# Spikes of the first feed-forward layer: eight GpSimd comparisons or two ScalarE activations

## The chip, the cores and the metric

The kernel runs on one core of one Trainium2 chip. The time is that of the device for one execution, in microseconds, from the first to the last instruction and what lies around them; lower is better.

## The reference

The input x has 16 sequences of 512 steps with 256 features. The first block projects x with Wr, Wk and Wv and runs each result through leaky neurons over time:

```
v = v + (x_t - v) * 0.5
s = (v - 1.0 >= 0)
v = v * (1 - s)
```

With the spikes r, k, v of the three it computes h = 0.9 h + k v and y = r h, projects y with Wo, adds x and normalises (x1). The feed-forward layer takes h1 = x1 W1 + b1 (1024 columns), runs it through the same neurons to the spikes s1, takes h2 = s1 W2 + b2, runs the neurons again, adds x1 and normalises; then x is added once more and normalised (x3). The second block is a mixture of 8 experts of 256 by 256 of which each token takes the best two, weighted by a softmax, added to x3 and normalised.

## The kernel before

Time is cut into 32 chunks of 16 steps; a chunk has 16 x 16 = 256 columns (step, sequence). Features lie on the 128 partitions. The kernel is a pipeline written out by hand: beat k (from -2 to 38) works at each stage on a chunk that is some beats behind. Beats 7 to 32 have all stages and are called steady (`edge` is false). All engines have their own instruction stream, ordered by `beat`, and wait for one another by semaphores with counts that depend on k.

The neurons of all layers run together on VectorE: `U` (two slots, used in turn) holds for each of the 16 steps 256 columns: 6 x 16 for r, k, v, 8 x 16 for h1, 2 x 16 for h2. Each step is one `membrane` (L710, U = 0.5 V + U) and one `reset` (L717, V = U where U is under the threshold). Halving is left out of the sums, so that the threshold is 2.0. Between these 32 instructions the lists STEADY, FILL and DRAIN place everything else that VectorE does, by slot numbers from 0 to 31. In STEADY the five steps of y stand in slots 0 to 4 (L747, L751, L757, L762, L766, L768), the sum z (L734) in slot 5, x3_low (L823) in slot 30.

y goes to TensorE, which multiplies it with Wo (`attn`, L378). TensorE's order in a steady beat: expert 0, the first of three r/k/v projections, attn, the transpose of z, the two other projections, w2 (L397, the product of the spikes s1 with W2), the transpose of x1, experts 1 to 3, w1, expert 4, the transpose of x3 (read by ScalarE as x3_hi, L534, and by VectorE as x3_lo, L823), the transpose of the gates, experts 5 to 7. Products are made with weights and data split in a high and a low part.

ScalarE moves the products out of PSUM: `to_lif` (L534 and L546) writes them into the slot of U for the next beat, `read_expert` (L583) writes weighted expert outputs to `term`, `normalised` (L597) applies the last layer norm, and L681 issues the DMA of the result. The beat of ScalarE begins with `to_lif` of the three projections, which waits for y, since it overwrites what y reads.

GpSimd's queue in a steady beat: the spikes s1 of the chunk (`spikes_h1`, eight instructions L1084, one for each 128 of the 1024 columns, 256 wide, from a strided view of U), then the DMA that adds term 4 of the chunk before to `acc` (`add_even`, L1102), the DMA that adds term 5 to `odd_sum` (`add_odd`, L1113), the bias on xb (`add_bias`, two instructions L1120), and between further DMAs the reciprocal deviations (L1070, L1072), the low part of x1 (L1127, two) and, last, the low part of x (L1091).

In the edge beats the spikes are made by VectorE (L1012).

Of the kernel before, what the change touches and what calls it, by code (L numbers as in the profile page):

```python
# [26 lines left out]
ALU = mybir.AluOpType  # L27
ACT = mybir.ActivationFunctionType

P = 128  # L30
B, T, D, F, E = 16, 512, 256, 1024, 8
STEPS = 16
N = STEPS * B
CHUNKS = T // STEPS
TILES = N // P
DK = D // P
FK = F // P
RKV_TILES = 3 * DK
EPS = 1e-5
THRESHOLD = 2.0  # L40
DECAY = 0.9


COL_H1 = RKV_TILES * B
COL_H2 = COL_H1 + FK * B
# [6 lines left out]
LAG_S = 3  # L52
# [54 lines left out]
class Beat:  # L107
# [15 lines left out]
    @property  # L123
    def dve_spikes(self):

        return FK if self.edge else 0

    def value(self, per, lag, add=0):

# [29 lines left out]
def some(n):  # L159

    return n > 0


def build(nc, x_T, x_tok, w_rkv, w_o, w_1, w_2, w_e0, w_e, consts, out):
    with ExitStack() as ctx:
        def sb(name, shape, dt=F32):
            return ctx.enter_context(nc.sbuf_tensor(name, shape, dt))

        def sem(name):
            return ctx.enter_context(nc.semaphore(name))  # L170


        wrkv_raw = sb("wrkv_raw", [P, 3, DK * D])
        wrkv_hi, wrkv_lo = sb("wrkv_hi", [P, 3, DK * D], F32R), sb("wrkv_lo", [P, 3, DK * D], F32R)
        wo = sb("wo", [P, DK, D])
        w1_hi, w1_lo = sb("w1_hi", [P, DK * F], F32R), sb("w1_lo", [P, DK * F], F32R)
# [8 lines left out]
        bias_stack = sb("bias_stack", [STACK, D], F32R)  # L185
        decay = sb("decay", [P, DK * B, STEPS])
        neg_half = sb("neg_half", [P, TILES])

        U = sb("U", [P, 2, STEPS, COLS])
        V = sb("V", [P, COLS])  # L190
# [60 lines left out]
        y_steps, attn_done, ln1_steps = sem("y_steps"), sem("attn_done"), sem("ln1_steps")  # L251
        x1T_done, x1_ready = sem("x1T_done"), sem("x1_ready")
        x1_hi_ready, x1_lo_ready = sem("x1_hi_ready"), sem("x1_lo_ready")
        s1_ready = sem("s1_ready")
        z_ready, zT_done, xb_ready = sem("z_ready"), sem("zT_done"), sem("xb_ready")
        ln2_steps, ln3_steps = sem("ln2_steps"), sem("ln3_steps")
        x3T_done, x3_hi_ready, x3_lo_ready = sem("x3T_done"), sem("x3_hi_ready"), sem("x3_lo_ready")
# [274 lines left out]
        def _(act):  # L532
# [3 lines left out]
            def to_lif(b, fill, col, tiles, bias):  # L536
# [11 lines left out]
                                                ACT.Identity, bias=cst[:, bias + e:bias + e + 1])  # L548
                last.then_inc(proj_read, 1)

            def read_x1(b):

                slot = b.slot(LAG_Y, 4)
                act.wait_ge(x1T_done, b.value(1, LAG_Y, 1))

                if some(b.value(2, LAG_Y + 4, 2)):
                    act.wait_ge(z_ready, b.value(2, LAG_Y + 4, 2))
                if some(b.fills()):
                    act.wait_ge(proj_filled, b.fills())
                for k in range(DK):  # L560
                    if k == 1 and b.has(LAG_M):
                        read_expert(b, 1)
                    for dst, done in ((x1_hi[:], x1_hi_ready), (x1[:, slot], x1_ready)):
                        nc.scalar.activation(dst[:, k, :], ps_attn[:, k, :], ACT.Identity,  # L564
                                             bias=cst[:, C_BE1 + k:C_BE1 + k + 1],
                                             scale=cst[:, C_G1 + k:C_G1 + k + 1]).then_inc(done, 1)
# [43 lines left out]
            def beat(b):  # L610
                if b.k == LAG_M:
                    act.wait_ge(split_lo, PIECES)
                fill = 0
                if b.has(LAG_RKV):

                    if b.has(LAG_Y):
                        act.wait_ge(y_steps, b.value(Y_STEPS, LAG_Y, Y_STEPS))
                    for f in range(3):
                        to_lif(b, f, 2 * f * B, 2, None)
                    fill += 3  # L620
                if b.has(LAG_M):

                    act.wait_ge(gate_steps, b.value(GATE_STEPS, LAG_M, 7))
                    nc.scalar.activation(gexp[:], gdiff[:], ACT.Exp).then_inc(gexp_ready, 1)
                if b.has(LAG_S):

                    if b.has(LAG_Z):
                        act.wait_ge(z_ready, b.value(2, LAG_Z, 2))
                    to_lif(b, fill, COL_H2, 2, C_B2)
                    fill += 1  # L630
                if b.has(LAG_Y):
                    read_x1(b)
                elif b.has(LAG_M):
                    read_expert(b, 1)
                if b.has(LAG_M):
                    read_expert(b, 2)
                if b.has(LAG_Y):

                    if b.has(LAG_S):
                        act.wait_ge(s1_ready, b.value(FK, LAG_S, FK))  # L640
                    for f in (0, 1):
                        to_lif(b, fill + f, COL_H1 + 2 * f * B, 2, C_B1 + 2 * f)
                if b.has(LAG_M):
                    read_expert(b, 3)
                if b.has(LAG_Y):
                    to_lif(b, fill + 2, COL_H1 + 4 * B, 2, C_B1 + 4)
                if b.has(LAG_Z):
                    norm_x3(b)
                if b.has(LAG_Y):
                    to_lif(b, fill + 3, COL_H1 + 6 * B, 2, C_B1 + 6)  # L650
                if b.has(LAG_M):
                    read_expert(b, 4)
                if b.k == LAG_RKV:
                    act.wait_ge(consts_loaded, 16)
                    copy(bias_stack[:], bias_raw).then_inc(bias_hi_ready, 1)
                    act.wait_ge(vec_set, 5)
                if b.has(LAG_Z):
                    act.wait_ge(x3T_done, b.value(1, LAG_Z, 1))

                    if some(b.value(E - 1, LAG_Z + 2, E - 1)):  # L660
                        act.wait_ge(expert_done, b.value(E - 1, LAG_Z + 2, E - 1))
                    copy(x3_hi[:, b.slot(LAG_Z, 2)], ps_zx[:]).then_inc(x3_hi_ready, 1)
                if b.has(LAG_M):
                    act.wait_ge(gateT_done, b.value(1, LAG_M, 1))
                    if some(b.value(1, LAG_M)):
                        act.wait_ge(bias_done, b.value(1, LAG_M))
                    copy(gate_T[:], ps_attn[0:STACK, :, 0:P]).then_inc(gateT_ready, 1)
                if b.has(LAG_X):
                    split_x(b)
                if b.k == LAG_X:  # L670
                    for f in range(3):
                        act.wait_ge(wrkv_loaded[f], 16)
                        copy(wrkv_hi[:, f, :], wrkv_raw[:, f, :]).then_inc(wrkv_hi_ready, 1)
                if b.has(LAG_M):
                    for e in (5, 6, 7):
                        read_expert(b, e)
                if b.has(LAG_F):
                    act.wait_ge(fin_steps, b.value(FIN_STEPS, LAG_F, FIN_STEPS))
                    normalised(3, res, res).then_inc(res_ready, 1)
                    act.wait_ge(res_ready, b.value(1, LAG_F, 1))  # L680
                    act.dma_start(out[b.chunk(LAG_F)], res[:]).then_inc(out_stored, 16)  # L681
                for p in pieces_in(b.k):
                    _, hi, _, n = pieces_of(p)
                    act.wait_ge(raw_loaded[p % RAW_SLOTS], 16 * (p // RAW_SLOTS + 1))
                    copy(hi, term[:, p % RAW_SLOTS, 0:n]).then_inc(split_hi, 1)
# [6 lines left out]
        def _(dve):  # L692
# [312 lines left out]

            def spikes_h1(b):


                if some(b.w2_fills()):
                    dve.wait_ge(proj_filled, b.w2_fills())  # L1010
                for ft in range(FK - b.dve_spikes, FK):
                    v.tensor_scalar(s1[:, ft, :].rearrange("p (t b) -> p t b", b=B),  # L1012
                                    U[:, (b.k - 1) % 2, :, COL_H1 + ft * B:COL_H1 + (ft + 1) * B],
                                    THRESHOLD, None, ALU.is_ge).then_inc(s1_ready, 1)

# [48 lines left out]
        def _(pool):  # L1064
# [6 lines left out]
                pool.wait_ge(rstd_ready[ln], b.value(2, lag, 1))  # L1071
                g.tensor_tensor(rstd[ln][:], veps[ln][:], neg_half[:], ALU.pow).then_inc(rstd_ready[ln], 1)  # L1072

            def spikes_h1(b, part):

                if part == 0:

                    if some(b.value(2 * STEPS, 0)):
                        pool.wait_ge(lif, b.value(2 * STEPS, 0))
                    if some(b.w2_fills()):  # L1080
                        pool.wait_ge(proj_filled, b.w2_fills())
                for e in range(2):
                    ft = 2 * part + e
                    last = g.tensor_scalar(s1[:, ft, :].rearrange("p (t b) -> p t b", b=B),  # L1084
                                           U[:, (b.k - 1) % 2, :, COL_H1 + ft * B:COL_H1 + (ft + 1) * B],
                                           THRESHOLD, None, ALU.is_ge)
                last.then_inc(s1_ready, 2)

            def split_x(b):
                pool.wait_ge(x_hi_ready, b.value(1, LAG_X, 1))  # L1090
                g.tensor_tensor(x_lo[:], xt[:, b.slot(LAG_X, 2)], x_hi[:].bitcast(F32),  # L1091
# [38 lines left out]
            def beat(b):  # L1130


                has_y, has_z, has_m, has_f = (b.has(lag) for lag in (LAG_Y, LAG_Z, LAG_M, LAG_F))
                if b.has(LAG_S):
                    for part in range((FK - b.dve_spikes) // 2):
                        spikes_h1(b, part)
                if has_f:
                    add_even(b, LAG_F, 4)
                    add_odd(b, LAG_F, 5)
# [26 lines left out]
                                    ALU.subtract).then_inc(split_lo, 1)  # L1166

            g.memset(neg_half[:], -0.5).then_inc(pool_set, 1)
            pool.wait_ge(pool_set, 1)
            run_beats(beat)  # L1170


# [43 lines left out]
```

## Time and profile before

| | |
|---|---|
| median of 3 runs | 1124.46 us (1119.31 to 1125.79) |
| the profiled execution | 1122.8 us |
| its span | 1120.9 us |
| VectorE busy | 1024.0 us, 91% |
| TensorE busy | 958.6 us, 86% |
| GpSimd busy | 715.7 us, 64% |
| ScalarE busy | 545.4 us, 49% |
| the eight spikes a beat, L1084 | 223.2 us in 208 instructions |
| mean granted clock of TensorE | 0.946 of full |

In the profile PE is TensorE, PEld its weight loads, DVE VectorE, ACT ScalarE, POOL GpSimd and SP the engine that only issues DMAs; a q behind a name is the engine's queue. The busy time of a GpSimd or VectorE instruction includes time in which it stands still for the other. Arrows read from input to output, leftwards: `s<-U` writes s from U. A time in brackets is how long the engine had been idle, with what ended it.

### The profile page before, as it was taken

To read this page: it belongs to the slowest core of one execution; us is meant where nothing else is said; L and a number is where in the kernel's file an instruction comes from. 1 tells how busy PE (TensorE), PEld (TensorE's weight loads), DVE (VectorE), ACT (ScalarE), POOL (GpSimd) and SP (SyncE) were. 2 spreads that over 40 slices of the span, in tenths; PEclk is the share of its full clock that TensorE was granted. 3 is DMA by queue.
4 is the path that set the end of the run, shared out by engine and by line. 5 is a ranking of instruction groups with operands and counts; after the bars stand their busy time and mean duration, and the time that the engine had idled before them with its cause. 6 is when DMAs were issued, how large, how long until landed. Compare 5 with 4: busy or idle time off the path is not lost.

```text
span 1120.9 us, 21932 instructions
## 1 busy us (share of the span) xinstructions
PE 958.6 (86%) x7552; PEld 926.4 (83%) x7552; DVE 1024.0 (91%) x3257; ACT 545.4 (49%) x1270; POOL 715.7 (64%) x838
## 2 busy tenths in 40 slices
PE   3567679999999999999999999999999999889783
PEld 3456668888888998888888899888888998789783
DVE  6888998999999999999999999999999999998863
ACT  4223334455455555455455555445455555346353
POOL 5154432778777667777777776677777677774453
PEclk9768888999999999999999999999999999899997
DMA  6110002334343444434343444433333444335565
GB/s 200 33 48 29 29 29 48 66 77 94 81 87 74 90 86 89 89 69 95 81 87 75 90 95 85 85 86 77 78 80 79 95 86 82 71 75 105 105 114 112
DMA packets 49361, 91.31 MB, mean 81 GB/s; under 512 B 5473, under 2 KB 5473, under 8 KB 49249
## 3 DMA queue, kind: packets, MB, share of 16 engines
q0 software_dynamic: 27648, 50.34, 26.5%
q1 hardware_dynamic: 16992, 31.16, 8.8%
q10 hardware_dynamic: 4608, 8.39, 2.0%
q8 instruction: 60, 0.98, 0.4%
q14 instruction: 53, 0.43, 0.1%
HBM read 31.16 MB, written 8.39 MB: 35 GB/s over the span
## 4 chain that ended last, share of the span: by engine, by line
DVE 48%; PE 37%; issue 6%; POOL 4%; ACT 3%; DMA 2%; DVEq 0%; POOLq 0%; ACTq 0%
DVE U L710 11%; PE ps_e L342 10%; DVE V L717 9%; PE ps_proj L412 6%; PE ps_proj L397 6%; PE ps_proj L342 6%; PE ps_attn L378 4%; DVE stats L775 4%; DVE h L762 3%; DVE h L751 3%; PE ps_proj L418 3%; DVE y L768 2%; POOL x_lo L1127 2%; DVE x_lo L823 2%; DVE y L747 1%
## 5 line engine op out<-in xcount | busy, mean ns | idle before, releaser
L342 PE MATMUL ps_e<-we_hi,x_hi 128*128 128x256 f32 (+1 forms) x1024 | 293.4, 287 | 6.3 <-ACT odd_sum L583 6.3
L710 DVE SCALAR_TENSOR_TENSOR U<-V,U 128x256 f32<-128x256 f32 (+5 forms) x656 | 275.4, 430 | 15.2 <-ACT U L546 7.6
L342 PE MATMUL ps_e<-we_lo,x_hi 128*128 128x256 f32 (+1 forms) x1024 | 287.1, 280 | 0.0
L342 PE MATMUL ps_e<-we_hi,x_lo 128*128 128x256 f32 (+1 forms) x1024 | 287.0, 280 | 0.0
L717 DVE SCALAR_TENSOR_TENSOR V<-U 128x256 f32<-128x256 f32 (+5 forms) x656 | 259.9, 406 | 1.0
L546 ACT ACTIVATE U<-ps_proj,cst 128x256 f32<-128x256 f32 x320 | 135.7, 482 | 195.7 <-PE ps_proj L418 101.8
L1084 POOL TENSOR_SCALAR s<-U 128x256 fp32r<-128x256 f32 x208 | 223.2, 1099 | 1.1 <-DVE V L717 1.1
L342 PEld LDWEIGHTS ps_e<-we_hi,x_hi 128*128 128x128 f32 x1024 | 193.5, 189 | 7.3 <-ACT odd_sum L583 7.3
L342 PEld LDWEIGHTS ps_e<-we_hi,x_lo 128*128 128x128 f32 x1024 | 194.8, 190 | 0.1
L342 PEld LDWEIGHTS ps_e<-we_lo,x_hi 128*128 128x128 f32 x1024 | 193.5, 189 | 0.0
L583 ACT ACTIVATE term<-ps_e,gate 128x256 f32<-128x256 f32 x384 | 161.8, 476 | 51.1 <-PE ps_e L342 49.5
L534 ACT ACTIVATE U<-ps_proj 128x512 f32<-128x512 f32 x96 | 57.5, 599 | 259.5 <-PE ps_proj L342 173.3
L1070 POOL TENSOR_SCALAR veps<-mv 128x2 f32<-128x2 f32 x128 | 44.5, 348 | 201.9 <-DVE mv L781 201.9
L378 PE MATMUL ps_attn<-wo,y 128*128 128x256 f32 x256 | 77.3, 454 | 86.2 <-DVE y L768 86.2
L412 PE MATMUL ps_proj<-x_hi,w_hi 128*128 128x256 f32 x512 | 136.4, 288 | 6.1 <-ACT x_hi L564 6.1
L378 PEld LDWEIGHTS ps_attn<-wo,y 128*128 128x128 f32 x256 | 54.0, 222 | 100.1 <-DVE y L768 74.5
L412 PE MATMUL ps_proj<-x_hi,w_lo 128*128 128x256 f32 x512 | 135.1, 286 | 0.0
L342 PE MATMUL ps_proj<-x_hi,wrkv_hi 128*128 128x256 f32 x384 | 113.8, 296 | 11.9 <-DVE wrkv_lo L1053 6.1
L418 PE MATMUL ps_proj<-x_lo,w_hi 128*128 128x256 f32 x512 | 106.8, 289 | 18.9 <-POOL x_lo L1127 18.9
L397 PE MATMUL ps_proj<-s,w_hi 128*128 128x256 f32 x512 | 121.5, 281 | 0.3 <-POOL s L1084 0.3
L397 PE MATMUL ps_proj<-s,w_lo 128*128 128x256 f32 x512 | 120.8, 280 | 0.0
L1127 POOL TENSOR_TENSOR x_lo<-x,x_hi 128x256 fp32r<-128x256 f32 x64 | 69.2, 1083 | 71.7 <-ACT x L564 71.5
(89 smaller groups left out, 2396.0 us busy)
## 6 DMA issues: line engine op xcount, KB each, us to landing
acc<-term POOLq DMA_DIRECT2D x96, 256.0 KB, 3.5
odd_sum<-term POOLq DMA_DIRECT2D x96, 256.0 KB, 3.4
xt<-x_T SPq DMA_DIRECT2D x33, 256.0 KB, 3.0
xa<-x_tok SPq DMA_DIRECT2D x32, 256.0 KB, 4.3
xb<-x_tok SPq DMA_DIRECT2D x32, 256.0 KB, 2.7
out<-res ACTq DMA_DIRECT2D x32, 256.0 KB, 2.1
term<-w SPq DMA_DIRECT2D x8, 256.0 KB, 5.3
term<-w_e SPq DMA_DIRECT2D x7, 256.0 KB, 2.9
```

The source lines that it names most:

```text
L342: mm = pe.matmul(dst, lhs, rhs, start=(i == 0), stop=(i == n - 1))
L378: mm = pe.matmul(ps_attn[:, j, :], y[:, k * N + j * P:k * N + (j + 1) * P], wo[:, k, :], start=(k == 0), stop=(k == DK - 1))
L397: mm = pe.matmul(ps_proj[:, bank, e, :], wp[:, c:c + P], s1[:, ft, :], start=(ft == 0 and part == 0), stop=(ft == FK - 1 and part == 1))
L412: pe.matmul(ps_proj[:, bank, e, :], wp[:, cols(k, e)], x1_hi[:, k, :], start=(k == 0 and wp is w1_hi), stop=False)
L418: mm = pe.matmul(ps_proj[:, bank, e, :], w1_hi[:, cols(k, e)], x1_lo[:, k, :], start=False, stop=(k == DK - 1))
L534: return nc.scalar.activation(out_, in_, ACT.Identity)
L546: last = nc.scalar.activation(dst[:, :, col + e * B:col + (e + 1) * B], ps_proj[:, bank, e, :].rearrange("p (t b) -> p t b", b=B), ACT.Ide ...
L583: last = nc.scalar.activation(dst[:, j * D:(j + 1) * D], ps_e[:, bank, j, :], ACT.Identity, scale=gate[:, b.slot(LAG_M, 2), j, e:e + 1])
L710: v.scalar_tensor_tensor(out=U[:, s, t, c0:c1], in0=V[:, c0:c1], scalar=0.5, in1=U[:, s, t, c0:c1], op0=ALU.mult, op1=ALU.add).then_inc(do ...
L717: v.scalar_tensor_tensor(out=V[:, c0:c1], in0=u, scalar=THRESHOLD, in1=u, op0=ALU.is_lt, op1=ALU.mult).then_inc(done, 1)
L1084: last = g.tensor_scalar(s1[:, ft, :].rearrange("p (t b) -> p t b", b=B), U[:, (b.k - 1) % 2, :, COL_H1 + ft * B:COL_H1 + (ft + 1) * B], T ...
L1127: g.tensor_tensor(x1_lo[:, k, :], x1[:, b.slot(LAG_Y, 4), k, :], x1_hi[:, k, :].bitcast(F32), ALU.subtract).then_inc(x1_lo_ready, 1)
```

## The change

In the steady beats the spikes s1 are made by ScalarE in two instructions over all 2048 columns. The first is Relu(U - (2 - 2^-23)) into a new buffer, `s1_excess`; it is above zero just where U is at least 2, as 2 - 2^-23 is the next smaller float. The second is its Sign, which is 1 or 0, into s1. Both stand at the beginning of ScalarE's beat, ahead of `to_lif`, and wait for the end of the scan before and for the last w2. A semaphore, s1_above, stands between them. GpSimd's `spikes_h1` and its call are gone, so its beat begins with `add_even` of term 4. `s1_excess` takes the place of `wrkv_raw`, whose three raw weights lie in its first part. A memset of the bias column is added at the start of GpSimd. The edge beats keep VectorE's spikes.

```diff
+BELOW = THRESHOLD - 2.0 ** -23
...
     @property
     def dve_spikes(self):
-        return FK if self.edge else 0
+        return self.edge
...
-        wrkv_raw = sb("wrkv_raw", [P, 3, DK * D])
+        s1_excess = sb("s1_excess", [P, FK * N])
+        wrkv_raw = s1_excess[:, 0:3 * DK * D].rearrange("p (f c) -> p f c", f=3)
...
+        neg_below = sb("neg_below", [P, 1])
...
+            def spikes_h1(b):
+                if b.k == FIRST_STEADY:
+                    act.wait_ge(pool_set, 2)
+                act.wait_ge(lif, b.value(2 * STEPS, 0))
+                if some(b.w2_fills()):
+                    act.wait_ge(proj_filled, b.w2_fills())
+                u = U[:, (b.k - 1) % 2, :, COL_H1:COL_H2].rearrange("p t (f b) -> p f t b", b=B)
+                spikes = s1[:].rearrange("p f (t b) -> p f t b", b=B)
+                above = s1_excess[:].rearrange("p (f t b) -> p f t b", f=FK, b=B)
+                nc.scalar.activation(above, u, ACT.Relu, bias=neg_below[:, 0:1]).then_inc(s1_above, 1)
+                act.wait_ge(s1_above, b.value(1, FIRST_STEADY, 1))
+                nc.scalar.activation(spikes, above, ACT.Sign).then_inc(s1_ready, FK)
...
                 fill = 0
+                if b.has(LAG_S) and not b.dve_spikes:
+                    spikes_h1(b)
                 if b.has(LAG_RKV):
...
             def spikes_h1(b):
-                for ft in range(FK - b.dve_spikes, FK):
+                for ft in range(FK):
...
-            def spikes_h1(b, part):
-                if part == 0:
-                    if some(b.value(2 * STEPS, 0)):
-                        pool.wait_ge(lif, b.value(2 * STEPS, 0))
-                    if some(b.w2_fills()):
-                        pool.wait_ge(proj_filled, b.w2_fills())
-                for e in range(2):
-                    ft = 2 * part + e
-                    last = g.tensor_scalar(s1[:, ft, :].rearrange("p (t b) -> p t b", b=B),
-                                           U[:, (b.k - 1) % 2, :, COL_H1 + ft * B:COL_H1 + (ft + 1) * B],
-                                           THRESHOLD, None, ALU.is_ge)
-                last.then_inc(s1_ready, 2)
...
-                if b.has(LAG_S):
-                    for part in range((FK - b.dve_spikes) // 2):
-                        spikes_h1(b, part)
                 if has_f:
                     add_even(b, LAG_F, 4)
                     add_odd(b, LAG_F, 5)
...
+            g.memset(neg_below[:], -BELOW).then_inc(pool_set, 1)
```

## Rows read from the trace of the kernel before

**Rows 1.** Two beats: us; busy PE PEld DVE ACT POOL; clock, DMA share, GB/s.

```profile
482.20:513.20 31.00, 28.64 (x239) 27.95 (x238) 30.11 (x93) 16.60 (x41) 22.82 (x28) 1.00 0.40 86
354.00:386.40 32.40, 30.06 (x238) 29.37 (x237) 30.40 (x93) 16.46 (x40) 22.53 (x28) 0.95 0.39 82
```

**Rows 2.** Timeline of PE: start, duration, instruction, count, idle before.

```profile
519.61 1.99 PE L378 MATMUL ps_attn<-wo,y 128*128 128x256 f32 x8 [2.34 <-DVE y L768]
```

**Rows 3.** Timeline of ACT, where x3 is copied.

```profile
541.01 0.60 ACT L534 ACTIVATE x_hi<-ps_zx 128x512 fp32r<-128x512 f32 x1
541.49 0.38 ACT L534 ACTIVATE gate_T<-ps_attn 72x256 fp32r<-72x256 f32 x1
```

**Rows 4.** Timeline of DVE from L823 to the end of y.

```profile
541.76 0.68 DVE L823 TENSOR_TENSOR x_lo<-ps_zx,x_hi 128x512 fp32r<-128x512 f32 x1
...
544.13 0.61 DVE L747 TENSOR_SCALAR y<-U 128x512 f32<-128x512 f32 x1
...
545.01 1.40 DVE L751 SCALAR_TENSOR_TENSOR h<-U,y 128x512 f32<-128x512 f32 x1
546.33 0.63 DVE L710 SCALAR_TENSOR_TENSOR U<-V,U 128x256 f32<-128x256 f32 x1
...
547.34 1.41 DVE L762 TENSOR_TENSOR_SCAN h<-decay,h 128x512 f32<-128x512 f32 x1
548.67 0.55 DVE L710 SCALAR_TENSOR_TENSOR U<-V,U 128x256 f32<-128x256 f32 x1
...
549.24 1.28 DVE L768 SCALAR_TENSOR_TENSOR y<-U,h 128x256 f32<-128x256 f32 x2
```

**Rows 5.** Timeline of POOL in the same stretch.

```profile
542.48 1.45 POOL L1091 TENSOR_TENSOR x_lo<-xt,x_hi 128x512 fp32r<-128x512 f32 x1 [0.73 <-ACT x_hi L534]
543.90 8.53 POOL L1084 TENSOR_SCALAR s<-U 128x256 fp32r<-128x256 f32 x8
552.38 0.89 POOL L1102 DMA_DIRECT2D acc<-term  x1
```

**Rows 6.** Timeline of DVE in an edge beat, the same steps of y.

```profile
132.85 0.41 DVE L747 TENSOR_SCALAR y<-U 128x512 f32<-128x512 f32 x1
133.29 1.25 DVE L751 SCALAR_TENSOR_TENSOR h<-U,y 128x512 f32<-128x512 f32 x1
...
134.83 1.22 DVE L762 TENSOR_TENSOR_SCAN h<-decay,h 128x512 f32<-128x512 f32 x1
...
136.19 1.11 DVE L768 SCALAR_TENSOR_TENSOR y<-U,h 128x256 f32<-128x256 f32 x2
```

**Rows 7.** Timeline of DVE while L1102 (521.41) and L1113 (522.04) are issued.

```profile
521.27 0.41 DVE L710 SCALAR_TENSOR_TENSOR U<-V,U 128x256 f32<-128x256 f32 x1
...
521.72 0.79 DVE L717 SCALAR_TENSOR_TENSOR V<-U 128x256 f32<-128x256 f32 x1
```

**Rows 8.** Timeline of DVE beside both L1120 (209.49 to 211.54), first steady beat.

```profile
210.13 0.93 DVE L710 SCALAR_TENSOR_TENSOR U<-V,U 128x256 f32<-128x256 f32 x1
...
211.14 0.69 DVE L717 SCALAR_TENSOR_TENSOR V<-U 128x256 f32<-128x256 f32 x1
```

**Rows 9.** Timeline of POOL and DVE in a beat near the end.

```profile
1035.89 0.86 POOL L1113 DMA_DIRECT2D odd_sum<-term  x1 [2.03 <-DMA odd_sum<-term]
...
1036.31 1.99 DVE L734 SCALAR_TENSOR_TENSOR z<-U,x 128x256 f32<-128x256 f32 x1
1036.46 1.55 POOL L1120 TENSOR_TENSOR xb<-xb,cst 128x256 f32<-128x256 f32 x2
```

**Rows 10.** Timeline of ACT around the beginning of its beat.

```profile
516.03 0.34 ACTq L681 DMA_DIRECT2D out<-res  x1
519.58 0.60 ACT L534 ACTIVATE U<-ps_proj 128x512 f32<-128x512 f32 x1 [3.58 <-DVE y L768]
523.58 0.60 ACT L534 ACTIVATE U<-ps_proj 128x512 f32<-128x512 f32 x1 [3.40 <-PE ps_proj L342]
```

**Rows 11.** Groups of ACT by form: busy us, mean ns, idle before.

```profile
L546 ACT ACTIVATE U<-ps_proj,cst 128x256 f32<-128x256 f32 x320 | 135.7, 482 | 195.7 <-PE ps_proj L418 101.8 <-PE ps_proj L397 93.9
...
L534 ACT ACT_TABLE_LOAD x1 | 1.3, 1283 | 0.7 <-PEq L1206 0.7
```

More of the change, by code:

```diff
@@ L253, in build @@
         x1_hi_ready, x1_lo_ready = sem("x1_hi_ready"), sem("x1_lo_ready")
-        s1_ready = sem("s1_ready")
+        s1_above, s1_ready = sem("s1_above"), sem("s1_ready")
         z_ready, zT_done, xb_ready = sem("z_ready"), sem("zT_done"), sem("xb_ready")
@@ L1168, in _ @@
             g.memset(neg_half[:], -0.5).then_inc(pool_set, 1)
-            pool.wait_ge(pool_set, 1)
+            g.memset(neg_below[:], -BELOW).then_inc(pool_set, 1)
+            pool.wait_ge(pool_set, 2)
             run_beats(beat)
```

## The prediction

> **What bounds the kernel now.** I read the windows of single beats first. A steady beat lasts 31.0 us where TensorE is granted its full clock and 32.4 us where the mean is 0.95. VectorE is busy for 30.1 us of the first, TensorE for 28.6, GpSimd for 22.8, ScalarE for 16.6 [rows 1]. So VectorE looks like the bound, and whoever lightens it or what slows it seems to win. The timelines show that this holds for one part of the beat only. Follow one round:
>
> - TensorE has idled 2.34 us for y (L768) when it starts the attention product at 519.61 [rows 2]. This is its one long wait in a beat: 28.6 busy and 2.3 idle make the 31.0. From there to the transpose of x3 it works without a pause.
> - ScalarE copies that transpose into x3_hi (L534 at 541.01, 0.60 long, over at 541.61) [rows 3], and VectorE takes x3_lo from it (L823) at 541.76 [rows 4]. VectorE got there 0.15 us after the copy was ready: it and TensorE arrive there together.
> - From L823 VectorE needs 8.76 us until the second L768 ends at 550.52 (549.24 + 1.28) [rows 4]; then TensorE may go on.
>
> So the loop is: y, some 22.1 us of TensorE and ScalarE, L823, 8.76 us of VectorE (I call it the tail), y. **What VectorE saves between y and L823 gives at most 0.15 us a beat, since TensorE isn't there sooner. What it saves or loses in the tail counts in full.** The eight spike instructions of GpSimd (L1084 x8, 543.90 to 552.43) cover the tail from 2.1 us after its start [rows 5].
>
> **The change, part by part.** It holds for the 26 beats 7 to 32.
>
> *GpSimd's eight spikes go.* In the tail VectorE's steps are longer than they are by themselves. With spikes beside them [rows 4], and in a beat without [rows 6]: L747 0.61 and 0.41; L751 1.40 and 1.25; L762 1.41 and 1.22; the pair L768 1.28 and 1.11. L710 takes 0.63 and 0.55 there, and 0.41 where nothing disturbs it [rows 7]. The differences are 0.20, 0.15, 0.19, 0.17, 0.22 and 0.14: 1.07 us a beat. The short steps between them I take at nothing. Each spike instruction holds up about one VectorE step by about 0.2 us, though it is itself 1.07 us long. Bounds: 0.9 (the edge beat's durations vary a little) to 1.3 (the short steps pay too).
>
> The Trainium skill (SBUF — State Buffer, Who interferes with whom) says that a VectorE instruction with two SBUF inputs and a GpSimd one that reads SBUF exclude each other for the whole instruction, whichever starts first, and that ScalarE never waits on anyone. By the first half eight spikes would cost VectorE up to their 8.5 us; the trace shows 1.07, so the sum goes by the trace.
>
> *What stood behind the spikes on GpSimd comes forward.* This is the part that decides. In its queue follow, without a wait that is still open at that time, the two accumulating DMA issues of terms 4 and 5 (L1102, L1113) and the two bias additions on xb (L1120). They run now from 552.38 on [rows 5], after y, where a loss costs nothing. Without the spikes they start when L1091 ends, at 543.9: in the tail, at L747, all four within some 3 us, and there nearly each VectorE step (L747, L717, L751, L710, L757, L717, L762) reads two SBUF inputs or is as sensitive. No DMA has to be waited for: the terms are written by then and the sums before them have landed. What they cost a VectorE step that stands behind them:
>
> - a DMA issue: L717 takes 0.79 instead of 0.41 with only L1102 and L1113 beside it [rows 7]: 0.38. Twice: 0.76.
> - the two additions: L710 0.93 and L717 0.69 instead of 0.41 [rows 8]: 0.52 + 0.28 = 0.80.
> - in a beat near the end L1113 and both additions follow each other as they will here, and the step L734, which has 256 columns as L710 and L717 have (0.41 undisturbed [rows 7]), takes 1.99 [rows 9]: 1.58 for three of the four; with a first DMA issue 1.96.
>
> So the four cost 1.56 by their parts and 1.96 by the nearest sequence. From below: today the four of them cost VectorE some 0.8 in a stretch where fewer of its steps are sensitive; from above 2.2, if each DMA issue also holds up a step in full before that sequence. I take 1.6, since in the tail there is a sensitive step behind each of them, and keep 0.8 to 2.2.
>
> *ScalarE's two instructions.* Rows give 0.38 for 256 columns, 0.60 for 512 [rows 3, 10]: 0.86 ns a column, so 1.92 us for 2048, and 0.1 more for one with a bias column (0.482 for 256 columns [rows 11]): 2.0 + 1.9 + 0.1 between them = 4.0 us. Bounds 3.9 and 5.3 (with one load of tables, below). ScalarE's last work of the beat before is the DMA issue at 516.03 to 516.37, then it idles 3.58 us for y, copies a projection at 519.58 (0.60) and idles again 3.40 us [rows 10]. The spikes fill the first of these gaps and overrun it by 0.4 to 0.9 us. Behind them is that copy, and for it waits TensorE's third projection, which can't start before the one ended at 523.5 (ScalarE's next copy waits for it [rows 10]). So the copy may end at 523.5 where it ended at 520.2: 3.3 us of cover, less 0.9. The product w2 needs the spikes later still. Price on the path: nothing; without that cover 4 us a beat. ScalarE waits for the last reset of the scan, long past, and for its own Relu.
>
> *After y*: VectorE loses the 0.8 us of the four instructions and 0.2 of spikes on L734 there. It will stand idle about 1 us at L823 instead. Worth 0.05 us of the 0.15 in a beat at full clock.
>
> *The rest*: one memset, one more semaphore, a shared buffer whose first use is over long before beat 7, VectorE's edge beats as they were: nothing; they lie beside the first load of weights or change no instruction.
>
> **Sum.** A beat: -1.07 + 1.60 - 0.05 = +0.48 us; times 26: +12.5 us. The profiled execution took 1122.8 us (its span is 1120.9), so it becomes 1135.3; the median of the runs is 1124.46, 0.15% higher. Forecast: 1136 us, 1.0% slower. What a measurement of this kernel can tell is 0.5%, 5.6 us, that is 0.22 us a beat: slower needs a price of the four above 1.34, faster one below 0.90.
>
> **Rivals.**
>
> 1. *The moved instructions cost little, and the kernel is faster.* If they share the SBUF port with VectorE better than in rows 8 and 9, or two of them fall beside steps that don't mind, they cost the 0.8 of today: -0.32 a beat, -8.3 us, 1116. It speaks for it that most DMA issues in the trace lie beside VectorE steps of normal length; against, that the sequence itself appears in rows 9 with its highest price. If they cost nothing: -1.12 x 26 = -29 us, 1095. The mechanism with its place: the tail of each steady beat; it decides below 0.90 us for the four. Chance 0.25. The Trainium skill (same page, same section) supports it: descriptors of a GpSimd DMA are said to need the write side of the port, which a two-input step doesn't take; then the two issues cost nothing. The trace has a row against it, the 0.79 of L717 [rows 7].
> 2. *Both cancel*: the four cost 0.90 to 1.34, for instance one issue 0.38 and the additions 0.80. 1119 to 1130, middle 1125. Chance 0.22.
> 3. *ScalarE comes too late.* Sign or Relu may lie in another table set than Exp; the one load of tables in the trace takes 1.28 us [rows 11]. One such load makes 5.3 us, still covered. From 6.5 us on (516.37 to 522.9) TensorE waits for the copy. Both instructions at half speed would do it: 7.8 us, 1.3 a beat more than the cover, on top of the sum: 1136 + 34 = 1170. Nothing in the rows speaks for it: copies that write U with the same stride take the 0.60 of others. Chance 0.03.
>
> **Chances and range.** The forecast's own case (price of the four 1.34 to 2.2) gets 0.50 and runs from 1130 to 1151. Slower in all 0.53, same 0.22, faster 0.25. The range leaves out rival 3, the cheapest part of rival 1 and the top of the forecast's case: 1112 to 1150.
>
> **What the profile of the changed kernel would show.** If the steps hold: in a steady beat L1102, L1113 and both L1120 right behind L1091; L747, L751 or L710 long by 0.4 to 1.6 us there, and L710 and L762 late in the tail at 0.41 and 1.22; from L823 to the end of y 9.3 us instead of 8.76; idle time of about 1 us before L823, ended by ScalarE's x3_hi, in each steady beat; TensorE's wait for y at 2.8 us instead of 2.3; two ACT instructions of 1.9 to 2.0 us, over before 0.9 us after y; steady beats of 31.4 us at full clock. A tail under 8.6 us makes rival 1 right. If VectorE does not idle at L823, the loop is read wrongly, and the savings after y count too: then up to 1 us a beat less than I say. TensorE waiting before the third projection would be rival 3. A changed share of beats at the lower clock (1.4 us each) would move the sum by itself.

## The result and the profile after

The changed kernel takes 1162.43 us (median of 4 runs, 1158.99 to 1167.81) against 1121.88 us for the one before: ratio 1.037, 95% interval 1.030 to 1.044. It is slower, as forecast, but by 3.7% where 1.0% was forecast. The profiled execution took 1158.99 us, its span is 1157.1.

In the changed kernel the line numbers are shifted: L842 is x3_lo (before L823), L766 to L787 the steps of y (L747 to L768), L729 and L736 the scan (L710, L717), L381 the product with Wo (L378), L1094, L1105, L1116 and L1123 are GpSimd's x_lo, the two DMA issues and the bias additions (L1091, L1102, L1113, L1120). In the kernels of the experiments some lines stand one to three further down. The stretch from x3_lo to the end of y, on VectorE's timeline:

```profile
524.42 0.69 DVE L842 TENSOR_TENSOR x_lo<-ps_zx,x_hi 128x512 fp32r<-128x512 f32 x1 [0.65 <-ACT x_hi L537]
...
526.80 0.87 DVE L766 TENSOR_SCALAR y<-U 128x512 f32<-128x512 f32 x1
527.59 1.13 DVE L736 SCALAR_TENSOR_TENSOR V<-U 128x256 f32<-128x256 f32 x1
528.63 1.59 DVE L770 SCALAR_TENSOR_TENSOR h<-U,y 128x512 f32<-128x512 f32 x1
530.15 0.87 DVE L729 SCALAR_TENSOR_TENSOR U<-V,U 128x256 f32<-128x256 f32 x1
...
531.40 1.22 DVE L781 TENSOR_TENSOR_SCAN h<-decay,h 128x512 f32<-128x512 f32 x1
532.53 0.40 DVE L729 SCALAR_TENSOR_TENSOR U<-V,U 128x256 f32<-128x256 f32 x1
...
532.95 1.08 DVE L787 SCALAR_TENSOR_TENSOR y<-U,h 128x256 f32<-128x256 f32 x2
```

and GpSimd's in the same stretch:

```profile
525.26 1.34 POOL L1094 TENSOR_TENSOR x_lo<-xt,x_hi 128x512 fp32r<-128x512 f32 x1 [1.59 <-ACT x_hi L537]
526.54 0.87 POOL L1105 DMA_DIRECT2D acc<-term  x1
527.13 1.18 POOL L1116 DMA_DIRECT2D odd_sum<-term  x1
527.80 2.93 POOL L1123 TENSOR_TENSOR xb<-xb,cst 128x256 f32<-128x256 f32 x2
```

The later steps have the lengths of the undisturbed beat [rows 6]: the spikes' 0.2 us each are gone. But L766, L736, L770 and L729 run beside the four moved instructions and take 0.87, 1.13, 1.59 and 0.87 us where they take 0.41, 0.41, 1.28 and 0.42 us when the four stand behind y: 0.46 + 0.72 + 0.31 + 0.45 = 1.9 us. 18 of 24 rounds look like this one; in five others L770 pays most of it (2.63 to 3.12 us), and in one the four cost 0.9 us. The stretch is 9.61 us long (524.42 to 534.03) instead of 8.76 [rows 4], and VectorE had idled 0.65 us for x3_hi before it.

ScalarE, with the two new instructions (L564, L566) and the copy behind them:

```profile
529.84 0.34 ACTq L700 DMA_DIRECT2D out<-res  x1
530.28 2.00 ACT L564 ACTIVATE s_excess<-U,neg_below 128x2048 f32<-128x2048 f32 x1 [0.47 <-ACT res L614]
532.38 1.91 ACT L566 ACTIVATE s<-s_excess 128x2048 fp32r<-128x2048 f32 x1
534.19 0.58 ACT L537 ACTIVATE U<-ps_proj 128x512 f32<-128x512 f32 x1
539.66 0.60 ACT L537 ACTIVATE U<-ps_proj 128x512 f32<-128x512 f32 x1 [4.89 <-PE ps_proj L345]
```

They are over 0.26 us after y, and the copy 0.74 us after it. There is still one load of tables in the whole trace. TensorE's timeline shows what I had not priced, the lower clock behind the wait for y: the product with Wo takes 3.42 us where it took 1.99 in [rows 2]:

```profile
534.08 3.42 PE L381 MATMUL ps_attn<-wo,y 128*128 128x256 f32 x8 [3.00 <-DVE y L787]
```

and the windows of two beats, and of three stretches around that wait (columns as in [rows 1]; the clock is the last but two):

```profile
494.90:526.80 31.90, 28.93 (x238) 28.46 (x237) 30.36 (x93) 20.33 (x42) 14.43 (x20) 1.00 0.40 83
526.80:560.40 33.60, 30.61 (x238) 29.64 (x237) 30.28 (x92) 20.36 (x42) 14.95 (x20) 0.95 0.38 79
```

```profile
531.00:534.00 3.00, 0.09 (x1) 0.00 (x0) 3.00 (x9) 2.91 (x2) 0.00 (x0) 1.00 0.27 88
534.90:536.90 2.00, 2.00 (x7) 1.56 (x6) 1.53 (x5) 0.00 (x0) 0.00 (x0) 0.50 0.00 0
538.00:541.00 3.00, 3.00 (x27) 3.00 (x26) 3.00 (x18) 0.60 (x1) 0.29 (x1) 1.00 0.32 87
```

TensorE idles 3.0 us, and then works for some 3 us at the lower of its two levels (0.50, 1.2 GHz) before it has 1.00 (2.4 GHz) again. Such a beat takes 33.6 us; one without takes 31.9 or 32.0.

I timed the 24 rounds from the end of y in beat 7 to that in beat 31, from the times of the single instructions. A round is the sum of y to x3_hi (the end of ScalarE's copy), then 0.03 to 0.6 us until VectorE's x3_lo starts, then x3_lo to the end of y. "TensorE waits for y" is its idle time just before the product with Wo; "low" counts the rounds in which its granted clock falls to 0.50. The columns of times are means over the 24 rounds, in us.

Each ratio is to executions of the kernel before that were made beside it (medians 1121.21 to 1127.10 us for the experiments). Ratios compare fast executions alone: two of the eleven of the kernel before with the changed buffers, 1365.10 and 1887.55 us, were far slower than the rest and are left out.

| kernel | time, us | ratio to before (95%) | y to x3_hi | x3_lo to y | TensorE waits for y | low |
|---|---|---|---|---|---|---|
| before | 1121.88 | 1 | 22.64 | 8.76 | 2.31 | 8 |
| changed | 1162.43 | 1.037 (1.030, 1.044) | 23.41 | 9.56 | 2.96 | 16 |
| four wait for y | 1095.02 | 0.972 (0.966, 0.977) | 22.52 | 7.67 | 1.09 | 0 |
| additions wait for y | 1085.26 | 0.964 (0.959, 0.970) | 22.30 | 7.68 | 1.06 | 0 |
| DMA issues wait for y | 1113.52 | 0.989 (0.983, 0.994) | 22.44 | 8.57 | 1.95 | 2 |
| additions first | 1110.96 | 0.987 (0.981, 0.993) | 22.59 | 8.57 | 1.95 | 4 |
| one DMA issue in front | 1149.30 | 1.023 (1.018, 1.029) | 23.13 | 9.30 | 2.71 | 12 |
| changed, TensorE busy | 1127.69 | 1.002 (0.999, 1.005) | 22.32 | 9.43 | 0.94 | 0 |
| before, TensorE busy | 1112.91 | 0.990 (0.984, 0.996) | 22.20 | 8.76 | 0.95 | 1 |
| changed, Relu twice | 1162.55 | 1.035 (1.029, 1.041) | 23.36 | 9.48 | 2.87 | 15 |
| next x split earlier | 1076.83 | 0.959 (0.953, 0.964) | 22.32 | 6.81 | 0.67 | 0 |
| the same, column at the end | 1073.48 | 0.956 (0.951, 0.961) | 22.04 | 6.79 | 0.90 | 0 |

In the two profiled executions a round after the change is 1.51 us longer on average than one before it, 36.2 us in 24. Of that 0.80 is the stretch before y, 0.71 the way from y to x3_lo.

### The profile page after: what moved, and what is told of

It reads as the page before. It is cut to its first block, busy times and chain, and to the rows that moved or that the text cites. A ratio compares the mean times of both kernels' runs of the same rounds, so it can differ in the third digit from the quotient of the medians.

```text
span 1157.1 us, 21803 instructions
## 1 busy us (share of the span) xinstructions
PE 982.8 (85%) x7552; PEld 951.5 (82%) x7552; DVE 1025.2 (89%) x3257; ACT 644.6 (56%) x1322; POOL 510.1 (44%) x631
## 4 chain that ended last, share of the span: by engine, by line
PE 56%; DVE 30%; issue 5%; ACT 3%; POOL 3%; DMA 2%; DVEq 0%; POOLq 0%; ACTq 0%
PE ps_e L345 15%; PE ps_proj L415 10%; PE ps_proj L400 9%; PE ps_proj L345 8%; DVE U L729 7%; PE ps_attn L381 7%; DVE V L736 6%; PE ps_proj L421 5%; DVE h L770 4%; DVE h L781 3%; POOL x_lo L1130 2%; PE ps_zx L389 2%; DVE y L766 2%; DVE x_lo L842 2%; DVE y L787 2%
## 5 line engine op out<-in xcount | busy, mean ns | idle before, releaser
L729 DVE SCALAR_TENSOR_TENSOR U<-V,U 128x256 f32<-128x256 f32 (+5 forms) x656 | 270.7, 423 | 13.4 <-ACT U L549 5.9
L736 DVE SCALAR_TENSOR_TENSOR V<-U 128x256 f32<-128x256 f32 (+5 forms) x656 | 258.8, 404 | 1.0
L1088 POOL TENSOR_SCALAR veps<-mv 128x2 f32<-128x2 f32 x128 | 40.7, 318 | 396.9 <-DVE mv L800 396.7
L381 PE MATMUL ps_attn<-wo,y 128*128 128x256 f32 x256 | 84.2, 486 | 97.8 <-DVE y L787 97.8
L381 PEld LDWEIGHTS ps_attn<-wo,y 128*128 128x128 f32 x256 | 56.8, 232 | 112.9 <-DVE y L787 89.0
L345 PE MATMUL ps_proj<-x_hi,wrkv_hi 128*128 128x256 f32 x384 | 118.3, 308 | 12.0 <-DVE wrkv_lo L1071 6.2
L400 PE MATMUL ps_proj<-s,w_hi 128*128 128x256 f32 x512 | 124.7, 284 | 0.0
L400 PE MATMUL ps_proj<-s,w_lo 128*128 128x256 f32 x512 | 124.3, 284 | 0.0
L1130 POOL TENSOR_TENSOR x_lo<-x,x_hi 128x256 fp32r<-128x256 f32 x64 | 74.2, 1162 | 95.3 <-ACT x L581 95.2
L345 PE MATMUL ps_proj<-x_hi,wrkv_lo 128*128 128x256 f32 x384 | 112.9, 294 | 0.0
```

The lines of the kernel that those rows point to most:

```text
L345: mm = pe.matmul(dst, lhs, rhs, start=(i == 0), stop=(i == n - 1))
L381: mm = pe.matmul(ps_attn[:, j, :], y[:, k * N + j * P:k * N + (j + 1) * P], wo[:, k, :], start=(k == 0), stop=(k == DK - 1))
L400: mm = pe.matmul(ps_proj[:, bank, e, :], wp[:, c:c + P], s1[:, ft, :], start=(ft == 0 and part == 0), stop=(ft == FK - 1 and part == 1))
L729: v.scalar_tensor_tensor(out=U[:, s, t, c0:c1], in0=V[:, c0:c1], scalar=0.5, in1=U[:, s, t, c0:c1], op0=ALU.mult, op1=ALU.add).then_inc(do ...
L736: v.scalar_tensor_tensor(out=V[:, c0:c1], in0=u, scalar=THRESHOLD, in1=u, op0=ALU.is_lt, op1=ALU.mult).then_inc(done, 1)
L1130: g.tensor_tensor(x1_lo[:, k, :], x1[:, b.slot(LAG_Y, 4), k, :], x1_hi[:, k, :].bitcast(F32), ALU.subtract).then_inc(x1_lo_ready, 1)
```

## Experiments

All but two start from the changed kernel. The edits act in beats 7 to 32 alone, but for the order of "additions first", which holds in every beat, and the places of buffers. All compute the whole reference.

**What the four instructions cost, and where.** GpSimd waits for y before all four:

```diff
+                if not b.edge:
+                    pool.wait_ge(y_steps, b.value(Y_STEPS, LAG_Y, Y_STEPS))
                 if has_f:
                     add_even(b, LAG_F, 4)
                     add_odd(b, LAG_F, 5)
                 if has_z:
                     add_bias(b)
```

> The changed kernel, but in the steady beats GpSimd waits for the end of y before it issues the two accumulating DMAs and the two bias additions. Theory A (those four instructions in the stretch before y cost VectorE 2.0 us a beat, the longer wait for y then costs TensorE its full clock in two beats of three): the stretch from x3_lo to the end of y is 7.6 us instead of 9.6, a steady beat 29.9 us, TensorE waits about 1.2 us for y and no beat shows a lowered clock; 1075 to 1092 us, faster than the kernel before. Rival B (ScalarE's two instructions are what holds up y or TensorE): the time stays at 1150 to 1165 us.

Measured: 1095.02 us, 2.8% faster than before; the stretch before y takes 7.67 us, so the removal of the spikes is worth 1.09 us there (8.76 - 7.67) and the four instructions cost 1.89 (9.56 - 7.67). TensorE waits 1.09 us and its clock never falls between beats. ScalarE's two instructions are in it as in the changed kernel: theory B falls. The time is 3 us above my range. VectorE now pays for the four after y and idles only 0.03 us on average at x3_lo, and x3_hi comes 22.52 us after y instead of 22.3; that the one brings about the other is my reading, no run shows it by itself.

The same wait between the DMA issues and the additions:

> The changed kernel, but only the two bias additions wait for the end of y in the steady beats; the two DMA issues stay first in GpSimd's beat. Theory A with equal shares (0.4 each issue, 0.5 to 0.7 each addition): the stretch from x3_lo to the end of y is 8.4 us, the beat 30.6, 1095 to 1115 us. If DMA issues cost a VectorE step nothing by themselves: the stretch is 7.7 us and the time that of the kernel in which all four wait.

The second case came for the stretch: 7.68 us, so a DMA issue that has no addition directly behind it costs VectorE nothing. The time did not follow it: 1085.26 us is 10 less than with all four behind y, since x3_hi comes after 22.30 us and not 22.52. L766 runs beside L1105 here and has its 0.41 us:

```profile
587.93 0.41 DVE L766 TENSOR_SCALAR y<-U 128x512 f32<-128x512 f32 x1
588.60 1.28 DVE L770 SCALAR_TENSOR_TENSOR h<-U,y 128x512 f32<-128x512 f32 x1
```

```profile
587.68 0.87 POOL L1105 DMA_DIRECT2D acc<-term  x1
588.46 0.98 POOL L1116 DMA_DIRECT2D odd_sum<-term  x1
593.33 2.35 POOL L1123 TENSOR_TENSOR xb<-xb,cst 128x256 f32<-128x256 f32 x2 [3.89 <-DVE y L787]
```

Now additions first in the beat, and the wait between them and the issues:

> The changed kernel, but in the steady beats the two bias additions come first in GpSimd's beat and the two DMA issues wait for the end of y. Theory A with equal shares: the stretch from x3_lo to the end of y is 8.6 us (two additions at 0.4 to 0.6), 1100 to 1120 us. If a DMA issue in front of the additions is what makes them dear, as the sequence near the end of the kernel before suggests, the two additions alone cost 0.8 us and this stretch is 8.4.

Measured: 8.57 us, the two additions alone cost 0.90. With issues 0 and additions 0.90, the 1.89 of all four is not their sum. The next kernel asks whether the order decides, without any wait:

```diff
+                if has_z:
+                    add_bias(b)
                 if has_f:
                     add_even(b, LAG_F, 4)
                     add_odd(b, LAG_F, 5)
-                if has_z:
-                    add_bias(b)
```

> The changed kernel, but GpSimd's beat begins with the two bias additions, and the two DMA issues follow, all four still in the stretch before y and without any added wait. If it is a DMA issue directly in front of the additions that makes them dear: the stretch from x3_lo to the end of y is 8.6 us, as with the additions alone, and the time 1110 to 1120 us. If the four cost the same in any order: 9.6 us and 1155 to 1165 us.

8.57 us, and 1110.96 us: two lines moved up turn 3.7% slower into 1.3% faster. VectorE's steps beside the additions:

```profile
514.42 0.86 DVE L766 TENSOR_SCALAR y<-U 128x512 f32<-128x512 f32 x1
515.20 0.86 DVE L736 SCALAR_TENSOR_TENSOR V<-U 128x256 f32<-128x256 f32 x1
515.98 1.28 DVE L770 SCALAR_TENSOR_TENSOR h<-U,y 128x512 f32<-128x512 f32 x1
```

Each addition holds up one step by 0.45 us; the issues that follow (515.72 and 516.31) leave L770 and what follows alone. And with one issue in front and one behind:

> The changed kernel, but the DMA issue of term 4 moves behind the additions in the steady beats: GpSimd's order before y is DMA of term 5, two additions, DMA of term 4. If one DMA issue directly in front of the additions makes a longer locked stretch: 9.1 to 9.6 us from x3_lo to the end of y, 1135 to 1160 us. If it takes two issues in a row: 8.6 us and 1105 to 1118 us, as with the additions first.

9.30 us on average, 1149.30 us. In 19 of the 24 rounds one step pays for all, in 13 of them L766:

```profile
523.37 2.25 DVE L766 TENSOR_SCALAR y<-U 128x512 f32<-128x512 f32 x1
525.54 0.41 DVE L736 SCALAR_TENSOR_TENSOR V<-U 128x256 f32<-128x256 f32 x1
```

```profile
523.19 0.88 POOL L1116 DMA_DIRECT2D odd_sum<-term  x1
523.80 1.53 POOL L1123 TENSOR_TENSOR xb<-xb,cst 128x256 f32<-128x256 f32 x2
```

L766 stands still from 523.4 until the second addition is nearly over, 1.83 us: VectorE doesn't get in between the issue and the additions. This is the picture of [rows 9], now in the middle of the kernel.

The order is not all of it, though. In three of the 24 rounds the stretch takes 8.57 to 8.59 us with the same order. There GpSimd waits for a term before the issue, so that issue and additions come while L770 is under way:

```profile
493.21 0.88 POOL L1116 DMA_DIRECT2D odd_sum<-term  x1 [0.98 <-ACT term L600]
493.82 2.30 POOL L1123 TENSOR_TENSOR xb<-xb,cst 128x256 f32<-128x256 f32 x2
```

```profile
493.09 1.28 DVE L770 SCALAR_TENSOR_TENSOR h<-U,y 128x512 f32<-128x512 f32 x1
...
494.75 0.87 DVE L736 SCALAR_TENSOR_TENSOR V<-U 128x256 f32<-128x256 f32 x1
495.55 1.66 DVE L781 TENSOR_TENSOR_SCAN h<-decay,h 128x512 f32<-128x512 f32 x1
```

L770 has its own length, and the additions cost 0.46 and 0.44 us as if no issue stood before them. Why the issue locks VectorE out in one case and not in the other stays open.

**What lowers the clock.** TensorE does 16 further products before it waits for y (their results are overwritten):

```diff
-                pe.wait_ge(y_steps, b.value(Y_STEPS, LAG_Y, Y_STEPS))
                 ...
+                if not b.edge:
+                    for i in range(16):
+                        pe.matmul(ps_attn[:, 0, :], wrkv_hi[:, 0, 0:P], x_hi[:, 0, :], start=True, stop=True)
+                pe.wait_ge(y_steps, b.value(Y_STEPS, LAG_Y, Y_STEPS))
```

> The changed kernel, but in the steady beats TensorE does 16 further products of 256 columns (about 1.9 us, results unused) just before it waits for y, so that it idles about 1.1 us instead of 3.0. GpSimd's order is that of the changed kernel. Theory A: the stretch before y stays at 9.6 us, but the granted clock stays full in all steady beats, so that 16 to 17 beats lose their 1.6 us: 1128 to 1138 us. Rival C (the lowered clock comes from elsewhere, as load or heat, not from the idle stretch): more work makes it no better, 1160 us or more.

Measured: 1127.69 us, just under the range; no low round of 24, y to x3_hi 22.32 us instead of 23.41. That is what the changed kernel takes too in its 8 rounds at full clock, 22.33, against 23.95 in the 16 others. More work on TensorE makes the kernel 35 us faster. Of this 1.09 a round (26 us in 24) is the clock; the rest is the stretch before y, shorter in some rounds (9.43 on average), and what lies outside these rounds.

```profile
556.46 2.08 PE L380 MATMUL ps_attn<-x_hi,wrkv_hi 128*128 128x256 f32 x16
...
559.55 1.99 PE L384 MATMUL ps_attn<-wo,y 128*128 128x256 f32 x8 [1.02 <-DVE y L790]
```

The kernel before with 12 such products:

> The kernel before, but in the steady beats TensorE does 12 further products of 256 columns (about 1.4 us, results unused) just before it waits for y, so that it idles about 0.9 us instead of 2.3. Theory A (the lowered clock follows the idle stretch): no steady beat shows a lowered clock, y to x3_hi takes 22.1 us on average instead of 22.6, 1105 to 1115 us. Rival C (load): the clock falls as often or more often, 1120 us or more.

1112.91 us, 1.0% faster than the kernel before: it too had paid for its wait, in 8 of 24 rounds. One low round is left where I expected none; it follows a wait of 1.75 us. Ordered by the mean wait for y the table reads: 0.7 to 1.1 us, 0 or 1 low rounds; 1.95, 2 and 4; 2.31, 8; 2.71, 12; 2.9 to 3.0, 15 and 16. Theory C, load or heat, falls. The length of the wait alone does not decide in the single round: in the kernel before waits of 2.34 to 2.46 us stand before low rounds and before full ones, in the changed kernel waits of 2.98 to 3.07. The longer wait makes the fall more frequent.

**ScalarE by itself.** The Relu twice:

```diff
-                nc.scalar.activation(above, u, ACT.Relu, bias=neg_below[:, 0:1]).then_inc(s1_above, 1)
-                act.wait_ge(s1_above, b.value(1, FIRST_STEADY, 1))
+                for i in range(2):
+                    nc.scalar.activation(above, u, ACT.Relu, bias=neg_below[:, 0:1]).then_inc(s1_above, 1)
+                    act.wait_ge(s1_above, b.value(2, FIRST_STEADY, i + 1))
```

> The changed kernel with the Relu done twice: ScalarE's spikes take 6 us instead of 4 in each steady beat. Theory A: the copy behind them ends 2 us later, still before TensorE's third projection, so nothing moves: ratio to the changed kernel within 0.5%, 1155 to 1168 us. Rival B (ScalarE's two instructions hold up the beat): 26 x 2 us more, about 1210 us.

1162.55 us against 1162.43: two more microseconds on ScalarE in each beat cost nothing. The copy behind them now ends 2.8 us after y.

```profile
564.10 4.04 ACT L565 ACTIVATE s_excess<-U,neg_below 128x2048 f32<-128x2048 f32 x2 [0.47 <-ACT res L615]
568.23 1.91 ACT L567 ACTIVATE s<-s_excess 128x2048 fp32r<-128x2048 f32 x1
570.05 0.58 ACT L537 ACTIVATE U<-ps_proj 128x512 f32<-128x512 f32 x1
573.50 0.60 ACT L537 ACTIVATE U<-ps_proj 128x512 f32<-128x512 f32 x1 [2.87 <-PE ps_proj L345]
```

**A faster version.** With the additions behind y the longest disturbance before y is L729 beside L1094, 1.30 us instead of 0.42. In the next kernel the additions stay behind y, and besides ScalarE splits the next x right behind the exponential (`gexp`), and GpSimd behind `split_x1`:

```diff
                     nc.scalar.activation(gexp[:], gdiff[:], ACT.Exp).then_inc(gexp_ready, 1)
+                if b.has(LAG_X) and not b.edge:
+                    split_x(b)
...
                 if has_y:
                     split_x1(b)
+                if b.has(LAG_X) and not b.edge:
+                    split_x(b)
```

> The changed kernel with the bias additions after y, and besides with the split of the next x in the middle of the steady beats (ScalarE's x_hi behind the exponential, GpSimd's x_lo behind the low part of x1) instead of at their end. It takes the 1.4 us GpSimd instruction, which holds up L710 by 0.88 us, out of the stretch before y. Theory A (the loop of y, TensorE, x3_hi, x3_lo, y): the stretch from x3_lo to the end of y is 6.8 us instead of 7.7; VectorE pays the 0.9 us after y, where it had 0.5 us to spare, so 0.4 to 0.5 us a beat are gained: 1070 to 1076 us. If VectorE's total is what counts, as where it has no time to spare: no change, 1085 us.

1076.83 us, 4.1% faster than before and 0.8 us above my range. The stretch before y is 6.81 us. VectorE now gets to x3_lo 0.49 us after x3_hi and no longer idles there: the loop has moved to VectorE alone, as expected.

**The remainder.** At full clock y to x3_hi takes 22.3 us in the kernels from the changed one (but for the one in which all four wait for y), and 22.1 in the two with GpSimd's spikes. From the start of one product of 256 columns to that of the next it is 118.5 ns on average in the changed kernel and 116.0 ns in the one before. Two kernels ask whether it is the place of the buffers: the kernel before with the buffers of the changed one,

> The kernel before with the buffers of the changed one (a first buffer of 2048 instead of 1536 columns, one more column behind neg_half), and not otherwise changed. It asks where the last 0.2 us a beat come from: with the changed kernel's buffers TensorE starts a product each 118.6 ns at full clock instead of 116.4. Theory D (the places of the operands in SBUF): 118.6 ns here too, y to x3_hi 22.3 us at full clock, about 0.1 to 0.2 us more a beat. Rival E (ScalarE's spikes or GpSimd's silence do it): 116.4 ns and 22.1 us as before.

and the fastest with the one-column buffer `neg_below` allocated last:

> The fastest kernel so far (additions after y, next x split in mid-beat) with the one-column buffer of the bias as the last allocation, so that all buffers between neg_half and the end lie 4 bytes lower again. Theory D in its narrow form (these 4 bytes shift data operands off a boundary): a product each 116.4 ns, y to x3_hi 22.1 us; since VectorE bounds this kernel, with 0.5 us between x3_hi and x3_lo, the time stays at 1072 to 1078 us. If the 2048 bytes of the first buffer or something else is the cause: 118.6 ns as now.

The first was 1.004 times the kernel before (1.0005 to 1.0076, 1126.24 against 1121.21 us), the size looked for, but with an interval that nearly reaches 1. Its profile is that of the execution of 1887.55 us, where products of 256 columns start each 223 ns though the granted clock is recorded as 1.00; it can't be set beside the others, so the question of that run, 118.6 or 116.4 ns, has no answer from its trace. The second has 116.5 ns where the kernel without this edit has 118.6, y to x3_hi 22.04 us instead of 22.32, and takes 1073.48 us. It differs from that kernel in the place of the 4-byte column alone, so this place is the cause of the slower start of products; the 2048 bytes of the larger first buffer, which stay, are not. Which operand minds it wasn't tried: by their lines the products of w1 fall to 117.4 and 117.7 ns only, the others to 115.4 and 116.4. VectorE is the bound, busy 28.6 of 29.5 us:

```profile
523.40:552.90 29.50, 28.46 (x238) 28.00 (x237) 28.61 (x93) 20.36 (x42) 14.45 (x20) 1.00 0.43 91
```

## Why the prediction was right or wrong

The direction was right, and so was the mechanism that I gave for it: the four instructions behind the spikes come into the stretch before y. The time was outside the range: 1162 against 1112 to 1150. (By its own numbers the forecast is 1137 us, 1124.46 + 12.5, and not 1136.) Point by point:

- **The loop** (y, TensorE, x3_hi, x3_lo, y) holds. VectorE idles 1.08 us on average at x3_lo, where "about 1 us" stood, and what it saved after y was lost there.
- **The spikes' price**, 1.07 us before y: measured 1.09.
- **ScalarE's instructions**, "4.0 us" and free: 2.00 + 1.91, with a gap of 0.1, done 0.26 us after y; free even with 2 us more, so the third rival has no part in it.
- **The four instructions, "I take 1.6"**: 1.89. Mis-sized by 0.3 us a beat, 8 us in all. My two figures were 1.56 by parts and 1.96 by the sequence near the end; the sequence was right, and the parts were wrongly read. I took the 0.38 us of L717 in [rows 7] for the price of an issue. The additions stand directly behind the issues there too:

```profile
521.41 0.89 POOL L1102 DMA_DIRECT2D acc<-term  x1
522.04 1.17 POOL L1113 DMA_DIRECT2D odd_sum<-term  x1
522.60 2.05 POOL L1120 TENSOR_TENSOR xb<-xb,cst 128x256 f32<-128x256 f32 x2
```

An issue has no price of its own; in front of the additions it doubled theirs in most rounds. The Trainium skill (SBUF — State Buffer, Who interferes with whom) says that a DMA's descriptors need the write side of the shared port, which a two-input step doesn't use. The issues alone agree with that, at 0: the two-input L770 takes its 1.28 us beside L1116. L766 has one input, so the 2.25 us that it takes beside an issue and two additions are not told by that sentence. Which side of the port is held between them no run here tells.

- **The clock had no term in the sum.** This is the step that failed, the largest of three misses. I wrote that TensorE's wait for y would grow to 2.8 us (it is 2.96), and of the lowered clock only that "a changed share of beats" would "move the sum by itself". The share went from 8 rounds of 24 to 16. From the two kernels with TensorE busy: at full clock y to x3_hi takes 22.09 us before and 22.32 after, so the lowered clock costs 0.55 us a round before (22.64 - 22.09) and 1.09 after (23.41 - 22.32), 13 us more in 24 rounds. The view to see it in was in my hands: [rows 1] show a beat at full clock and one at 0.95 that is 1.4 us longer, and I did not ask what TensorE did before it fell.
- **"The rest ... nothing"**: the changed buffers cost 0.2 us a round, 5 us. That they do so by the place of the 4-byte bias column is shown in the fastest kernel, where moving it gave 0.28 us back.

In 24 rounds: 19 us for the stretch before y (0.80 each, forecast 0.53), 13 for the clock, 5 for the column, and 1 back between x3_hi and x3_lo: the 36 measured. Against the forecast the misses are 8, 13 and 5 us, 26 on 1136.

The first rival, moved instructions that cost little, was wrong for this order, but is right for two others: additions first, 1110.96 us (they cost 0.90 of the 1.09 that the spikes gave back); additions behind y, 1085.26.

## What to carry to other kernels

When work is taken off an engine's queue, ask what runs in its place: here the removal was worth 1.09 us a round, and the instructions that moved up cost 1.89, until they were put behind y or only in another order. Find the loop that sets the period and which stretch of each engine lies in it; a microsecond of VectorE counted in full before y, and not at all after it as long as VectorE idled at x3_lo. And price a longer wait of TensorE twice, for itself and for the clock that follows it: a few products without use in the wait were worth 1% to 3%.

## What the runs showed of the hardware

- In the six kernels whose mean wait of TensorE for y is 1.1 us or less, its clock stayed at the full level in all but 1 of 144 rounds, and that one follows a wait of 1.75 us. In the two with a mean of about 2.9 us it fell to the lower level for some 3 us in 31 of 48. Waits of equal length were followed by a fall in some rounds and not in others.
- A GpSimd addition of 256 columns holds up one VectorE step by 0.45 us, a DMA issue alone by nothing. An issue directly followed by two additions held up one step by 1.5 to 1.8 us in one piece in 19 of 24 rounds, and cost no more than the additions in three.
- A buffer of 4 bytes a partition in front of TensorE's operands moved the mean distance of its products of 256 columns from 116.5 to 118.6 ns (1.8%).
